# Attention phase of a fused Flamingo-style block: the order of one iteration rewritten on four engines

## The reference

```python
x = x + tanh(g_xattn[0]) * xattn(layernorm(x), ctx, ctx, wq, wk, wv, wo)
x = x + tanh(g_ffn[0]) * ffn(layernorm(x), fast_b, w_fc, w_proj, u, v, gate)
x = x + tanh(g_xattn[1]) * align(ctx, layernorm(x))         # dynamic time warping
x = x + tanh(g_ffn[1]) * bitlinear_ffn(layernorm(x), w1, b1, w2, b2)

def xattn(query, key, value, wq, wk, wv, wo):
    q, k, v = (heads(a @ w.T) for a, w in ((query, wq), (key, wk), (value, wv)))
    attn = softmax(einsum('bhqd,bhkd->bhqk', q, k) / 16)
    return merge(einsum('bhqk,bhkd->bhqd', attn, v)) @ wo.T

def ffn(x, ...):                                              # ternary weights
    h = bitlinear(x, w_fc) + gate * (x @ v.T @ fast_b.T @ u.T)
    return bitlinear(relu(h) ** 2, w_proj)
```

## Time and profile before

| | |
|---|---|
| median of 3 runs | 1793.09 us |
| the profiled execution | 1793.27 us |
| its span, first to last instruction | 1791.5 us |
| busy: PE, PEld, DVE, ACT, POOL | 1369.3, 1064.1, 1488.4, 1145.1, 644.3 us |
| mean granted TensorE clock | 0.873 |

### The profile page before, as it was taken

How to read it: one execution, slowest core, us unless ns; L and a number is a source line. 1 busy time by engine, 2 the same in 40 slices (tenths; PEclk the granted TensorE clock), 3 DMA queues, 4 the chain that set the end, 5 groups by cost and what they waited for, 6 DMA issues and landing times. The chain is left out here.

```text
span 1791.5 us, 37525 instructions
## 1 busy us (share of the span) xinstructions
PE 1369.3 (76%) x11461; PEld 1064.1 (59%) x11461; DVE 1488.4 (83%) x4194; ACT 1145.1 (64%) x2463; POOL 644.3 (36%) x1094
## 2 busy tenths in 40 slices
PE   4799999999999999999999984233232005898996
PEld 3588888888888888888888764000000003566664
DVE  7678888888888887888878753999998998999995
ACT  4477777777777777777777752243334003999997
POOL 3233343433434334343343323100000003777785
PEclk8899999999999999999999996555555556999999
DMA  6444544445444454444444312222220003223221
GB/s 175 116 139 128 152 127 131 130 125 149 127 133 131 124 147 127 133 134 124 143 127 139 82 42 57 71 60 61 57 41 6 0 0 93 67 95 101 89 78 48
DMA packets 322942, 179.56 MB, mean 100 GB/s; under 512 B 93793, under 2 KB 318193, under 8 KB 322802
## 3 DMA queue, kind: packets, MB, share of 16 engines
q1 hardware_dynamic: 322802, 178.07, 35.6%
HBM read 122.91 MB, written 50.33 MB: 97 GB/s over the span
## 5 line engine op out<-in xcount | busy, mean ns | idle before, releaser
L741 ACT ACTIVATE pts<-s 128x512 f32<-128x512 f32 x512 | 281.7, 613 | 85.9 <-PE s L484 85.9
L1035 DVE TENSOR_REDUCE nmax<-s 128x2 f32<-128x512 f32 x512 | 327.3, 681 | 7.7 <-PE s L467 6.5
L1148 POOL TENSOR_TENSOR r<-rl 128x512 f32<-128x512 f32 x128 | 133.1, 1040 | 224.6 <-ACT rl L771 181.7
L467 PE MATMUL s<-kst,qst 96*128 96x256 bf16 x1024 | 164.2, 276 | 22.4 <-DMA qst<-q_parts_dram 9.7
L484 PE MATMUL s<-qst,kst 128*128 128x256 bf16 x1024 | 158.0, 276 | 1.4 <-ACT pts L741 0.8
L1426 PE MATMUL gate<-diag,one 128*128 128x512 f16 x35 | 21.2, 607 | 172.0 <-DVE left L1517 172.0
L771 ACT ACTIVATE rl<-wb,fscl 128x256 f32<-128x256 f32 x256 | 108.0, 477 | 64.7 <-PE wb L570 64.7
L566 PE MATMUL wb<-x2l,wfcT 128*128 128x256 f32 x512 | 143.4, 302 | 0.7 <-ACT dd L793 0.7
L498 PE MATMUL oacc<-pts,vw 128*32 128x256 f32 x2048 | 137.9, 387 | 1.3 <-ACT pts L741 1.2
L567 PE MATMUL wb<-x2h,wfcT 128*128 128x256 f32 x512 | 132.6, 281 | 0.0
L433 PE MATMUL wb<-wprT,r2l 128*128 128x256 f32 x512 | 129.3, 292 | 2.8 <-DVE r2l L1004 2.8
(11 more groups left out here) (304 smaller groups left out, 4629.8 us busy)
## 6 DMA issues: line engine op xcount, KB each, us to landing
kst<-k_parts_dram SPq DMA_DIRECT2D x384, 64.0 KB, 2.6
qst<-q_parts_dram SPq DMA_DIRECT2D x384, 64.0 KB, 2.4
k_parts_dram<-kp SPq DMA_DIRECT2D x32, 384.0 KB, 5.2
q_parts_dram<-qp SPq DMA_DIRECT2D x32, 384.0 KB, 3.1
xin<-in_x_dram SPq DMA_DIRECT2D x32, 256.0 KB, 3.1
cT_raw<-in_ctx_T_dram SPq DMA_DIRECT2D x32, 256.0 KB, 5.4
xres<-in_x_dram SPq DMA_DIRECT2D x32, 256.0 KB, 4.6
cin<-in_ctx_dram SPq DMA_DIRECT2D x32, 256.0 KB, 4.7
```

Source lines behind the costliest of these rows:

```text
L467: last = pe.matmul(s1[h % 2][:, t, :], qst[b.p][0:MAXROW, h, t * P:t * P + P], kst[b.p][0:MAXROW, h, :], start=True, stop=True)
L741: act.activation(pt[h % (2 * HPG)], s2[h % 2][:], ACT.Exp).then_inc(e["expd"], 1)
L1035: v.tensor_reduce(nmax[:, T * h:T * h + T], s1[h % 2][:], AX.X, ALU.max, negate=True)\
L1148: pool.tensor_tensor(r2[:], rl[:, k % 2], rl[:, k % 2], ALU.mult)\
```

## The change

The order of the blocks within an iteration is rewritten on TensorE, ScalarE, VectorE and GpSimd. No block is added, dropped or altered, and `values` keeps its four groups of four heads.

```diff
--- before.py
+++ after.py
@@ -601,32 +601,33 @@
                     scores2(i, 2, 4)
                 if there(z):
                     out_proj(z)
+                if there(i):
+                    scores2(i, 4, 6)
                 if there(a):
                     queries(a)
                 if there(i):
+                    scores2(i, 6, 8)
                     values(i, 0)
-                    scores2(i, 4, 6)
                 if there(s):
                     values_proj(s)
-                if there(i):
-                    scores2(i, 6, 8)
+                if there(y):
+                    turn_y(y)
                 if there(s):
                     scores1(s, 6, 8)
                 if first:
                     turn_fc(0, W_B, 3), turn_low(0, W_C, 4)
-                if there(y):
-                    turn_y(y)
+                if there(i):
+                    values(i, 1)
+                    scores2(i, 8, 10)
                 if there(z):
                     turn_xh2(z)
-                if there(i):
-                    values(i, 1)
                 if there(y):
                     turn_half(y)
                     products(y)
                 if there(z):
                     low_rank(z)
                 if there(i):
-                    scores2(i, 8, 10)
+                    scores2(i, 10, 12)
                 if there(s):
                     scores1(s, 8, 10)
                 if first:
@@ -636,7 +637,7 @@
                 if there(z):
                     fc(z, 0)
                 if there(i):
-                    scores2(i, 10, 12)
+                    scores2(i, 12, 14)
                 if there(s):
                     scores1(s, 10, 12)
                 if first:
@@ -644,16 +645,14 @@
                 if there(z):
                     fc(z, 1)
                 if there(i):
-                    scores2(i, 12, 14)
-                if there(s):
-                    scores1(s, 12, 14)
-                if there(i):
                     values(i, 2)
                     scores2(i, 14, 16)
                 if there(s):
+                    scores1(s, 12, 14)
+                if there(z):
+                    fc(z, 2)
+                if there(s):
                     scores1(s, 14, 16)
-                if there(z):
-                    fc(z, 2)
                 if there(i):
                     values(i, 3)
                 if there(s):
@@ -814,46 +813,47 @@
                 first = at(i, -1)
                 if first:
                     put_proj(0), put_proj(1), put_proj(2), put_proj(3)
+                if there(i):
+                    exps(i, 4, 6)
                 if there(a):
                     qh_copy(a)
                 if there(i):
+                    exps(i, 6, 8)
                     copy_group(i, 0)
-                    exps(i, 4, 8)
+                if there(s):
+                    values_copy(s)
                 if there(y):
                     yT_copy(y)
-                if there(s):
-                    values_copy(s)
+                if there(a):
+                    middle_part(a, "q_rem", qr, qp, "q_parts_mid")
+                if there(i):
+                    copy_group(i, 1)
                 if there(z):
                     xh2_copy(z)
                 if there(y):
                     half_copy(y)
-                if there(a):
-                    middle_part(a, "q_rem", qr, qp, "q_parts_mid")
-                if there(i):
-                    copy_group(i, 1)
+                if there(i):
+                    exps(i, 8, 10)
+                if there(z):
+                    low_copy(z)
+                if there(y):
+                    distance(y)
+                if there(i):
+                    exps(i, 10, 12)
                 if there(ct):
                     ctx_high(ct)
-                if there(y):
-                    distance(y)
-                if there(z):
-                    low_copy(z)
-                if there(i):
-                    exps(i, 8, 10)
                 if there(z):
                     relu(z, 0)
                 if there(i):
-                    exps(i, 10, 12)
+                    exps(i, 12, 14)
                 if there(z):
                     square(z, 0)
                     relu(z, 1)
                 if there(i):
-                    exps(i, 12, 14)
-                if there(z):
-                    square(z, 1)
-                if there(i):
                     copy_group(i, 2)
                     exps(i, 14, 16)
                 if there(z):
+                    square(z, 1)
                     relu(z, 2)
                     square(z, 2)
                 if there(i):
@@ -1051,10 +1051,10 @@
                     x_low(a)
                 if there(y):
                     low_squares(y, 3)
+                if there(s):
+                    maxima(s, 0, 2)
                 if there(a):
                     k_remainder(a)
-                if there(s):
-                    maxima(s, 0, 2)
                 if there(nx):
                     x_stats(nx)
                 if there(s):
@@ -1074,29 +1074,29 @@
                     v.tensor_scalar(ln_v[:, c], ln_mv[:, c, 1], EPS, None, ALU.add).then_inc(e["ln_var"], 1)
                 if there(s):
                     maxima(s, 4, 6)
+                if slots:
+                    w("ln_rstd", norms(i, 1), 2 * NB + 5)
+                if there(y):
+                    ln3(y)
                 if there(z):
                     residual1(z)
                     aggregate(2, 3)
                     c = slice(2 * T, 3 * T)
                     w("ln_rstd", norms(i, 0), 2 * NB + 5)
                     v.tensor_scalar(ln_v[:, c], ln_mv[:, c, 1], EPS, None, ALU.add).then_inc(e["ln_var"], 1)
-                if slots:
-                    w("ln_rstd", norms(i, 1), 2 * NB + 5)
-                if there(y):
-                    ln3(y)
                 if there(a):
                     q_remainder(a)
+                if there(y):
+                    y_low(y)
                 if there(z):
                     w("ln_rstd", norms(i, 2), 2 * NB + 5)
                     ln2(z)
+                if there(s):
+                    maxima(s, 6, 8)
+                if there(z):
+                    low_half(z)
                 if there(nx):
                     ln1(nx)
-                if there(y):
-                    y_low(y)
-                if there(z):
-                    low_half(z)
-                if there(s):
-                    maxima(s, 6, 8)
                 if there(z):
                     low_rank_half(z)
                 if there(s):
@@ -1179,10 +1179,10 @@
                 if there(a):
                     parts(a, "k_parts", kr, kp)
                 rstd(i)
-                if there(z):
-                    x1_rstd(i, z)
                 if there(y):
                     halves(y)
+                if there(z):
+                    x1_rstd(i, z)
                 if there(a):
                     parts(a, "q_parts", qr, qp)
                 if there(z):
```

More of the change, by code:

```diff
@@ L653, in iteration @@
                 if there(s):
-                    scores1(s, 14, 16)
+                    scores1(s, 12, 14)
                 if there(z):
                     fc(z, 2)
+                if there(s):
+                    scores1(s, 14, 16)
                 if there(i):
@@ L829, in iteration @@
                     half_copy(y)
-                if there(a):
-                    middle_part(a, "q_rem", qr, qp, "q_parts_mid")
-                if there(i):
-                    copy_group(i, 1)
-                if there(ct):
-                    ctx_high(ct)
-                if there(y):
-                    distance(y)
-                if there(z):
-                    low_copy(z)
                 if there(i):
@@ L842, in iteration @@
                 if there(z):
+                    low_copy(z)
[3 more added lines that the diff above has]
+                    exps(i, 10, 12)
+                if there(ct):
+                    ctx_high(ct)
+                if there(z):
                     relu(z, 0)
                 if there(i):
-                    exps(i, 10, 12)
+                    exps(i, 12, 14)
                 if there(z):
@@ L1181, in iteration @@
                 rstd(i)
+                if there(y):
+                    halves(y)
                 if there(z):
                     x1_rstd(i, z)
-                if there(y):
-                    halves(y)
                 if there(a):
```

## The result

The changed kernel takes 1887.9 us (1887.57 to 1888.76, 4 runs), the kernel before 1793.57 in the same comparison: a ratio of 1.0525 with a 95% interval of 1.0509 to 1.0541, or 94 us slower. The forecast was 1808 us, 1791 to 1820.

What follows compares the result with a forecast made beforehand. TensorE's own order was taken as the bound. New waits 1.37 plus restarts 0.20 plus scores 0.05 less old waits 1.08 gave +0.54 us an iteration, x 28 = +15.1 us: 1808 us, 8 in 10 within 1791 to 1820.

Steps and rivals of the forecast that it cites:

- the three old waits: TensorE waits at scores of heads 2 and 3 (0.31 us), turn_xh2 (0.35), fc 0 (0.42): 1.08 us an iteration.
- Chain A: From turn_y's start Y through yT's copy, y_low and ln2 to turn_xh2 at Y + 2.77: TensorE waits 0.36 us.
- The walk: The prediction's block-by-block timing of one iteration from traced lengths: +0.54 us an iteration.
- Chains A to D: Four new TensorE waits: turn_xh2 0.36 us, product with `ones` 0.41, ahead of fc 0 0.12, max_transpose 0.48; together 1.37.
- C: ScalarE's distance now behind low_copy; fc 0 overwrites the bank distance reads, so TensorE waits 0.12 us.
- D: values 2 and scores2 of heads 14, 15 moved earlier leave max_transpose less cover for the reduces: 0.48 us wait.
- rival 3: Slower by more: GpSimd's ctx_low makes low_squares 0 late, pushing head 12's reduce: +1.16 us an iteration, 1825 us, chance 0.07.

Runs made afterwards that it cites:

- filler run: The changed kernel with 16 more matmuls on TensorE just ahead of its wait for ln2 at turn_xh2: 1872.26 us, ratio 1.0429.
- GpSimd held back: The changed kernel with two waits added on GpSimd: q's third part waits for ln2, products_low for ln1; no order changed: 1819.34 us, ratio 1.0131.
- one beside it: The changed kernel with products_low ahead of q's third part on GpSimd, leaving one long subtraction beside ln2: 1841.65 us, ratio 1.0272.

## Why the prediction was wrong

Step by step, by its own list.

- **What bounds the kernel, and the three old waits**: right. Taking away two of them, 0.73 us by the prediction, shortened the period by 0.59 (31.85 to 31.26) and gave 18 us.
- **Chain A**: this step failed. "ln2 0.61 later ... and takes 0.73" took the length of ln2 from a place where nothing long ran beside it, and carried it to a place where two long GpSimd subtractions run. It measured 2.52. The walk gives no place at all to the middle part of q, which the change moves on ScalarE to directly behind the copy of yT, and so never asked when GpSimd's part behind it would start, and beside what. By the walk ln2 starts at Y + 1.99, and in the changed kernel it does (582.98 to 584.97); q's part starts at Y + 1.94 (584.92), where before it started at Y + 3.98 (510.15 to 514.13). Cost: the 53 us between the filler run (1872.3) and GpSimd held back (1819.3).
- **The clock**: no term of the sum. It follows from the same step: the forecast had a wait of 0.36 us at this place, and the runs in which TensorE idled 0.19 us (GpSimd held back) and 1.03 us (one beside it) there had a clock of 1.00 from 100 to 1010 us. About 16 us.
- **Chains A to D without these two**: right in place and nearly in size. GpSimd held back has 0.35 at turn_xh2 and 0.05 in the block behind it (0.36 forecast), 0.38 at `ones` (0.41), 0.31 ahead of fc 0 (0.12), 0.66 at max_transpose (0.48). C and D were a fifth of a microsecond too small each: a release by VectorE or ScalarE cost 0.05 at `xh`, but at max_transpose and fc 0 about 0.25. The period is 0.75 over before, not 0.54. The run is 25 us over before, where 15 was forecast; of the 27 us in its profiled execution the 28 steady intervals have 20.5 and the last one, which I had left out, 4.2.
- **The rivals**: rival 3 named GpSimd, but as a late supplier, not as a neighbour in SBUF. In the changed kernel low_squares 0 does wait for GpSimd (0.46 us, at 596.17), but head 12's reduce behind it then waits for TensorE's scores, so this did not fall on the path. Its +1.16 us should read 0.54 + 0.60 = +1.14.

The trace of the kernel before had shown the lock. One of the four subtractions at its start (L951), all of one shape, has a GpSimd subtraction beside it and takes twice as long as the next:

```profile
10.34 1.34 DVE L951 TENSOR_TENSOR wkTl<-osb,wkTh 128x512 fp32r<-128x512 f32 x1 [3.61 <-ACT wkTh L696]
11.61 0.68 DVE L951 TENSOR_TENSOR wqTl<-osb,wqTh 128x512 fp32r<-128x512 f32 x1
```

```profile
9.87 1.27 POOL L1137 TENSOR_TENSOR cTl<-cT_raw,cTh 128x512 fp32r<-128x512 f32 x1 [3.91 <-ACT cTh L701]
```

And halves is a row of tiny GpSimd instructions that stood beside the normalisations. One of its casts, before and after the change (ns, min/median/max):

```profile
L1173 POOL CAST hpb<-hrest x32: 187/251/253, 128.1 to 1101.6; 128x2 bf16<-128x2 f32 x32
```

```profile
L1173 POOL CAST hpb<-hrest x32: 187/188/188, 127.1 to 1194.5; 128x2 bf16<-128x2 f32 x32
```

251 against 188 ns for two elements per partition. In the kernel before, the 27 casts with ln1 beside them take 250 to 253, the 5 others 187 or 188: there it was the small instruction that stood behind VectorE.

The Trainium skill, SBUF — State Buffer (SBUF: two separate sides), has the rule for both directions: VectorE and GpSimd share one pair of SBUF ports by an exclusive lock. VectorE takes it in a 2-port mode, or with two inputs in SBUF against a GpSimd instruction that reads SBUF; whoever starts first has it for its whole instruction, and the other blocks. The traces agree on the lock: each half of ln2 ended 0.15 us behind the subtraction that it stood behind (586.22 behind 586.07, 587.49 behind 587.34). By which of the two conditions ln2 takes the pair no run shows.

What the neighbours cost could have been worked out from rows of the kernel before, as an estimate. On ScalarE the middle part of q starts 0.12 before the end of the copy of yT, which the walk had at Y + 1.34, and takes 0.63 us, so GpSimd's part can start near Y + 1.9 (it did at Y + 1.94). The two subtractions last 2.40 us together (514.13 to 516.53) and end at Y + 4.34, 1.62 behind the end of ln2 in the walk. 31 x 1.62 is 50 us more, near 1858. On top of the 1819 of the run with GpSimd held back it is 1869, where the filler run has 1872.

## What to carry to other kernels

When a block moves to another time, its duration moves with it only if its neighbours on the other engines are harmless: for each moved VectorE instruction whose tiles all lie in SBUF, list the GpSimd instructions that will run beside it, and the other way round, and price the pair as one after the other. Look for it in the min/median/max of small instructions: here one took 188 ns in one place and 251 in another, where it stood behind VectorE. And a long wait on TensorE can have a second price, its clock: here a wait of 1.98 us cost it in about half of the iterations, one of 1.03 us in none of the steady ones.

## What was not expected of the hardware

- Two VectorE halves of 0.40 us cost 1.8 us more beside two GpSimd subtractions; but two reduces from PSUM (`nmax`, 573.41, 1.29 us) kept their length beside `kp` (573.52 to 574.69), and so did, in the trace before, the statistics of an SBUF tile (`ln_st`, 499.91, 0.74 us, beside `kp` from 499.54 to 500.70). The eleven traces sort them. Held beside a long GpSimd instruction were `tensor_scalar` on SBUF tiles (ln1, ln2) and the subtraction of two SBUF tiles (`wkTl`, in every run). Never held were subtractions with one tile in PSUM (y_low, low_half, low_rank_half), reduces and the statistics.
- Speed is no sign of it. ln2 handles 256 elements per partition in 0.33 us, start to start, and a reduce from PSUM, never held, 512 in 0.60: ln2 is no faster per element and is held all the same.
- The clock fell behind a wait of about 2 us for `xh` in some iterations and not in others of the same length; with 16 matmuls in the wait it stayed at 1.00 from 100 to 1010 us, and the kernel was 15.6 us faster for doing more.
- A release costs TensorE 0.05 us in one place and about 0.25 in others. In the run with GpSimd held back, turn_xh2 starts at 587.88 behind `xh`'s end at 587.83, and max_transpose at 601.32 behind the last reduce's end at 601.07. Why they differ stays open.
